# Batch 0's keys and queries made in the last tiles of a top-2 expert stage, and a chain of small VectorE steps spread between other work

## The chip, the cores and the metric

The kernel runs on one core of a Trainium2 chip. The metric is the device time of one execution in microseconds (us), as the median of several. TensorE (PE) multiplies matrices, VectorE (DVE), ScalarE (ACT) and GpSimd (POOL) do the elementwise work, and the queue of SyncE (SPq) issues the DMAs.

## The reference

Eight steps follow one another on x, 16 batches of 112 rows by 256 values. Even steps are cross-attentions to a context of 375 rows for each batch, odd ones are feed-forward steps. This case is about the places where a top-2 expert step hands over to the next attention.

```python
x = x + tanh(g_xattn[0]) * L0_xattn(layernorm(x), ctx, ...)   # 16 heads of 16
x = x + tanh(g_ffn[0])   * L0_ffn(layernorm(x), ...)          # 8 experts, the best 2 kept
x = x + tanh(g_xattn[1]) * L1_xattn(layernorm(x), ctx, mask)  # scores clipped to +-100, masked
x = x + tanh(g_ffn[1])   * L1_ffn(layernorm(x), ...)          # 8 experts, the best 2 kept
x = x + tanh(g_xattn[2]) * L2_xattn(layernorm(x), ctx)
...                                                           # three more steps
# an attention, for each batch
q, k, v = xn @ wq + bq, ctx @ wk + bk, ctx @ wv + bv
out = softmax(q k^T / 4, per head) @ v @ wo + bo
# a top-2 step: gates from the logits, all experts computed, two of them weighted
```

## The kernel before

The program is a sequence of stages: attention 0, top-2 stage 0, attention 1, top-2 stage 1, attention 2, and three others. Each stage is a block in which every engine has its own instruction stream, and each block ends in a barrier of all engines. An engine waits for another by semaphores; inside a stage all orders are written out by hand.

An attention handles one batch in a turn, with a software pipeline over batches: turn i has the exponentials and the weighing of batch i (`on["e"]`), the scores and row maxima of batch i+1 (`on["m"]`), the keys and queries of batch i+2 (`on["p"]`), and the output of batch i-1 (`on["o"]`). `schedule` runs turns -3 to 16. A turn has 32 slots, and a `Plan` says at which slot each piece stands. For turns below 0 (`start`) the pieces are not spread over the slots: the keys come first, then the queries, then all scores. Keys and queries go through DRAM to be laid out by heads: PE makes keys (two products of 6 matmuls, `keys`) and queries (`L1258`), ACT and POOL or DVE split them into two fp16 parts (`L812`, `L1013`; in attention 1 `L806`, `L717`, `L719`; the queries `L823`, `L731`, `L733`), SPq writes them (`L620`, `L630`) and reads them back as stacks (`kst` at `L574`, `qst` at `L578`), and only then can PE make scores (`L1184`). DVE takes each score's row maximum (`L1053` or `L1057`); at the end of the turn PE turns the maxima (`L1273`).

A top-2 stage works on 14 tiles of 128 rows, again skewed: in iteration i PE makes the eight experts' products of tile i in four groups of six matmuls (`experts`), the logits of tile i+1 and the transposes of tile i+2. ACT scales four experts, DVE adds the other four (`L1483`), POOL sums and writes tile i (`L1425`), DVE takes its statistics in iteration i+1 (`L1505`). Bank 1 of PSUM holds the logits only. The reciprocal standard deviations that the next layer norm needs come from a Newton iteration of 13 small dependent DVE steps (`rstd_part`, called in one go by `row_rstd`): once at the end of iteration 0 for the tiles 10 to 13, and once at the end of iteration 13 for the first 11 batches, with the shifts and the first two normed batches behind them. Iterations 1 to 10 are a hardware loop of two iterations a trip, the others stand unrolled.

## Time and profile before

| | us |
|---|---|
| median of 3 executions (lowest, highest) | 1503.87 (1501.83, 1505.4) |
| the profiled execution's own time | 1508.3 |
| its span, first to last instruction | 1506.5 |
| busy in it: PE, DVE, ACT, POOL | 1343.4, 1118.5, 689.8, 417.6 |

The difference between own time and span, 1.8 us, lies around the instructions. Busy time is summed over the whole span; stages differ, so the places of the change are read from the timeline, which gives the start of each group of instructions in us from the span's start. The handovers that matter here lie at 395.4 (to attention 1) and 862.7 (to attention 2), the starts of the two top-2 stages at 292.6 and 753.8.

### The profile page before, as it was taken

To read this page: it belongs to the slowest core of one execution; us is meant where nothing else is said; L and a number is where in the kernel's file an instruction comes from. 1 tells how busy PE (TensorE), PEld (TensorE's weight loads), DVE (VectorE), ACT (ScalarE), POOL (GpSimd) and SP (SyncE) were. 2 spreads that over 40 slices of the span, in tenths; PEclk is the share of its full clock that TensorE was granted. 3 is DMA by queue.
4 is the path that set the end of the run, shared out by engine and by line. 5 is a ranking of instruction groups with operands and counts; after the bars stand their busy time and mean duration, and the time that the engine had idled before them with its cause. 6 is when DMAs were issued, how large, how long until landed. Compare 5 with 4: busy or idle time off the path is not lost. (4 is left out here: it accounts for less than half of the span.)

```text
span 1506.5 us, 36868 instructions
## 1 busy us (share of the span) xinstructions
PE 1343.4 (89%) x11864; PEld 980.0 (65%) x11864; DVE 1118.5 (74%) x3709; ACT 689.8 (46%) x1635; POOL 417.6 (28%) x588
## 2 busy tenths in 40 slices
PE   5799999799689899999789779999987997996998
PEld 2577887545356676776534348787876886883766
DVE  7688787578489888888678757767664775666997
ACT  2566676533234455554333236667662222332331
POOL 2233336244433344446124413333330000000000
PEclk8899999899889999999889979999999998997999
DMA  5444445311323233334010233333335441451000
GB/s 158 119 133 119 138 144 156 92 69 32 97 83 92 73 86 89 90 87 116 15 56 18 68 98 96 91 101 89 101 124 166 141 160 35 123 150 34 11 17 21
DMA packets 134832, 138.80 MB, mean 92 GB/s; under 512 B 38601, under 2 KB 122060, under 8 KB 134604
## 3 DMA queue, kind: packets, MB, share of 16 engines
q1 hardware_dynamic: 134716, 137.30, 31.7%
q8 instruction: 67, 1.10, 0.3%
q14 instruction: 49, 0.40, 0.1%
HBM read 101.77 MB, written 35.48 MB: 91 GB/s over the span
## 5 line engine op out<-in xcount | busy, mean ns | idle before, releaser
L1057 DVE TENSOR_REDUCE negm<-ps 112x1 f32<-112x375 f32 x512 | 260.1, 541 | 114.2 <-PE ps L1184 112.4
L777 ACT ACTIVATE p<-ps 125x448 f32<-125x448 f32 x432 | 229.3, 543 | 189.0 <-PE ps L1212 118.0
L1184 PE MATMUL ps<-kst,qst 96*112 96x375 f16 x768 | 236.1, 343 | 21.3 <-DMA qst<-q_split 9.4
L1199 PE MATMUL ps<-qst,kst 112*125 112x224 f16 (+1 forms) x1152 | 211.6, 266 | 8.3 <-POOL qst L747 4.3
L747 POOL TENSOR_TENSOR qst<-m_row,diag 16x448 f16<-16x448 f16 x128 | 130.0, 1043 | 283.6 <-ACT m_row L851 278.6
L1199 PEld LDWEIGHTS ps<-qst,kst 112*125 112x125 f16 (+1 forms) x1152 | 149.1, 139 | 45.1 <-issue 9.5
L1613 PE MATMUL ps<-fw,xs_e 128*128 128x512 f16 x672 | 167.5, 390 | 0.0
L1053 DVE CUSTOM_DVE_ANT_0 with_mask<-ps,mask_add 112x375 f16<-112x375 f32 x256 | 135.8, 546 | 19.9 <-issue 18.5
L1041 DVE TENSOR_SCALAR ps<-ps 125x448 f32<-125x448 f32 x192 | 120.9, 630 | 29.0 <-PE ps L1199 27.5
L1184 PEld LDWEIGHTS ps<-kst,qst 96*112 96x112 f16 x768 | 99.0, 133 | 53.9 <-DVE negm L1057 25.6
L1107 PE MATMUL ps<-ctxT,wkv_split 128*128 128x375 f16 (+1 forms) x576 | 118.6, 348 | 9.8 <-DVE ctxT L888 9.2
L1107 PE MATMUL ps<-wkv_split,ctxT 128*125 128x256 f16 x864 | 119.0, 275 | 0.8 <-DVE ks L1013 0.8
L1223 PE MATMUL ps<-p,v 125*32 125x112 f32 x3456 | 113.6, 265 | 1.5 <-ACT p L777 0.9
L747 POOL TENSOR_TENSOR mst<-m_row,mask_diag 32x448 f16<-32x448 f16 x64 | 64.5, 1036 | 162.3 <-ACT m_row L851 154.6
L1613 PEld LDWEIGHTS ps<-fw,xs_e 128*128 128x128 f16 x672 | 65.3, 100 | 66.0 <-issue 6.5
L1107 PEld LDWEIGHTS ps<-wkv_split,ctxT 128*125 128x125 f16 (+1 forms) x864 | 97.9, 137 | 2.8 <-DVE ks L1013 0.7
L1223 PEld LDWEIGHTS ps<-p,v 125*32 125x32 f32 x3456 | 81.3, 111 | 26.0 <-issue 17.8
L1212 PE MATMUL ps<-mst,mask_add 128*125 128x448 f16 x192 | 74.1, 395 | 24.6 <-DVE ps L1041 23.7
L1107 PEld LDWEIGHTS ps<-ctxT,wkv_split 128*128 128x128 f16 x576 | 58.7, 104 | 47.8 <-issue 23.0
L777 ACT ACTIVATE p_a<-ps 125x448 f32<-125x448 f32 x144 | 78.0, 543 | 22.1 <-PE ps L1212 14.9
L2345 PE MATMUL ps<-wgu,xqT 128*128 128x512 f32 (+3 forms) x224 | 72.4, 478 | 3.4 <-DVE xh L2274 2.0
L860 ACT ACTIVATE v<-ps 125x256 f32<-125x256 f32 x144 | 55.7, 387 | 26.1 <-PE ps L1107 21.6
(237 smaller groups left out, 2409.8 us busy)
## 6 DMA issues: line engine op xcount, KB each, us to landing
k_split<-ks SPq DMA_DIRECT2D x48, 375.0 KB, 3.5
kst<-k_split SPq DMA_DIRECT2D x96, 187.5 KB, 2.9
fw<-in_w SPq DMA_DIRECT2D x16, 1024.0 KB, 7.2
qst<-q_split SPq DMA_DIRECT2D x96, 112.0 KB, 2.4
kst<-k_split SPq DMA_DIRECT2D x96, 93.8 KB, 2.6
stage<-in_ctxT SPq DMA_DIRECT2D x16, 375.0 KB, 4.3
ctxn<-in_ctx SPq DMA_DIRECT2D x16, 375.0 KB
rows<-x SPq DMA_DIRECT2D x48, 112.9 KB, 2.6
```

What stands on the lines that cost most here:

```text
L747: pool.tensor_tensor(m_stack[q][m_rows, 4 * hg:4 * hg + 4, :], g.m_row[q][m_rows, :].rearrange("p (o s) -> p o s", o=1) .to_broadcast([n_m ...
L777: act.activation(p[P_OF[hg]][:, kt, :], ps[0:KR, BK_ST + n % 2, 0:4 * S], ACT.Exp).then_inc(s_exp, 1)
L1041: dve.tensor_scalar(st, st, -CLIP, CLIP, ALU.max, ALU.min).then_inc(s_clip, 1)
L1053: dve.tensor_tensor_reduce(g.with_mask[h % 2][:, :], scored, g.mask_add[1 - par][0:S, :], 1.0, -3e38, ALU.add, ALU.max, g.maxima[1 - par][ ...
L1057: dve.tensor_reduce(g.negm[1 - par][:, h:h + 1], scored, AX_X, ALU.max, negate=True).then_inc(s_max, 1)
L1107: mm = pe.matmul(out, lhs(l, c), rhs(r, c), start=(k == 0), stop=(k == 3 * KC - 1))
L1184: mm = pe.matmul(ps[0:S, BK_S + h % 2, 0:SK], g.q_stack[q][0:96, h, :], g.k_stack[q][0:96, h // 2, :], start=True, stop=True)
L1199: mm = pe.matmul(bank[:, 2 * r * S:2 * (r + 1) * S], g.k_stack[par][0:rows, pr, kt * KR:(kt + 1) * KR], g.q_stack[par][0:rows, 2 * pr:2 * ...
L1212: pe.matmul(bank, g.mask_add[par][:, kt * KR:(kt + 1) * KR], g.m_stack[par][:, 4 * hg:4 * hg + 4, :], start=False, stop=True, skip_group_c ...
L1223: mm = pe.matmul(pv[32 * j:32 * j + 32, hg * S:(hg + 1) * S], g.v[par][:, kt, 4 * hg + j, :], p[P_OF[hg]][:, kt, j * S:(j + 1) * S], start ...
L1613: mm = pe.matmul(out, lhs(l, c), rhs(r, c), start=(k == 0), stop=(k == 3 * KC - 1))
L2345: mm = pe.matmul(gate_up[w][:, first:last], xqT[:, c, :], wgu[:, w, c, first:last], start=(c == 0), stop=(c == KC - 1))
```

## The change

Batch 0's part of the first turns of attention 1 and 2 moves into the top-2 stage before it: in iteration 11 and 12 (NT is 14) PE makes the two key products in bank 1 (the logits' bank), in iteration 12 it turns batch 0's normed rows and in iteration 13 it makes the queries, with their copies, splits and DMA writes. The attention then begins at turn -1, with its pieces at the plan's slots, since `start` holds for attention 0 alone. The semaphores for these steps are shared by the stages (`FirstBatch`). The 13 steps of each `rstd` chain stand one by one at five places of each iteration, from iteration 0 (tiles) and from iteration 9 (batches 0 to 7 rather than 0 to 10). DVE makes the low half of the next tile (`xs`) before it finishes the gate weights, ACT copies the turned weights before it makes the exponentials, the split of the key and value weights moves from iteration 12 to 10, and the hardware loop covers iterations 3 to 8.

```diff
-        for i in range(-3, 5):
+        for i in range(-3 if first else -1, 5):
...
+                for e in range(2):
+                    sp.wait_ge(s_qdram[0][e], 16)
+                for c in range(2):
+                    stack_queries(sp, g, 0, c, s_stack[0][c])
                 read_batches(sp, g, layer - 1, 2, NT)
...
-                start = isinstance(i, int) and i < 0
+                start = first and isinstance(i, int) and i < 0
...
# top-2 stage, SyncE
+                    if isinstance(i, int) and i == NT - 1:
+                        held(sp, g, n0.khi, 2)
+                        held(sp, g, n0.klo, 2)
+                        store_keys(sp, g, 0, n0.kdram[0])
...
+                    if isinstance(i, int) and i == NT:
+                        held(sp, g, n0.qsplit, 1)
+                        for e in range(2):
+                            store_queries(sp, g, 0, e, n0.qdram[0][e])
+                        sp.wait_ge(n0.kdram[0], 16)
+                        for c in range(2):
+                            stack_keys(sp, g, 0, c, n0.stack[0][c])
...
# top-2 stage, VectorE
+                def part_of_rstd(i, k):
...
+                    first = 0 if i < 3 else NT - 5
+                    n = (i - first) * 5 + k
+                    if not 0 <= n < RSTD_PARTS:
+                        return
...
+                    if isinstance(i, int) and i in (NT - 3, NT - 2):
+                        m = i - NT + 3
+                        dve.wait_ge(n0.khi, m + 1)
+                        dve.scalar_tensor_tensor(out=g.k_split[0][:, m, 1, :], in0=ps[:, 1, 0:SK],
+                                                 scalar=g.bk[:, m:m + 1], in1=g.k_split[0][:, m, 0, :],
+                                                 op0=ALU.add, op1=ALU.subtract).then_inc(n0.klo, 1)
...
# top-2 stage, TensorE
                     if tiled(i + 1):
                         pe.wait_ge(s_xlo, i + 2)
+                        if isinstance(i, int) and i == NT - 2:
+                            pe.wait_ge(n0.klo, 1)
...
+                    if isinstance(i, int) and i in (NT - 3, NT - 2):
+                        m = i - NT + 3
+                        pe.wait_ge(s_wlo, 1)
+                        pe.wait_ge(s_lgsb, i + 2)
+                        split_products(ps[:, 1, 0:SK], lambda l, c: g.wkv_split[:, 0, l, c, m * 128:(m + 1) * 128],
+                                       lambda r, c: g.ctxT[:, r, c, 0:SK]).then_inc(n0.k, 1)
```

PE's instructions at the handover to attention 1, before: behind the last experts (`fw`) the barrier, the bias product (`wo,bv`), the keys (`ctxT,wkv_split`), transposes (`ident,xn`) and queries (`xnT,wq`).

```order
L1096 MATMUL ps<-wo,bv 1x256 [waits attention_weights1]
L1096 MATMUL ps<-wo,bv 1x256
L1107 MATMUL ps<-ctxT,wkv_split 128x375 x12
L1150 MATMUL ps<-ident,xn 128x112 [waits a0_bias_copied,a0_x_loaded3]
L1150 MATMUL ps<-ident,xn 128x112
L1258 MATMUL ps<-xnT,wq 128x112 [waits a0_ident]
L1258 MATMUL ps<-xnT,wq 128x112 x3
L1107 MATMUL ps<-ctxT,wkv_split 128x375 [waits a0_q_split]
```

These are the keys and queries of batch 0 and the first keys of batch 1; the scores (`L1184`, `kst,qst`) come 12 rows further on.

And the same place now:

```order
L1135 MATMUL ps<-wo,bv 1x256 [waits attention_weights1]
L1135 MATMUL ps<-wo,bv 1x256
L1223 MATMUL ps<-kst,qst 112x375 [waits a_stacked0_0]
L1189 MATMUL ps<-ident,xn 128x112 [waits a_q_scaled,a0_bias_copied,a_xn]
L1189 MATMUL ps<-ident,xn 128x112
L1146 MATMUL ps<-ctxT,wkv_split 128x375 x6
L1223 MATMUL ps<-kst,qst 112x375
L1223 MATMUL ps<-kst,qst 112x375 [waits a0_experts_high]
L1146 MATMUL ps<-ctxT,wkv_split 128x375 x6
L1223 MATMUL ps<-kst,qst 112x375 [waits a0_experts_high] x2
L1297 MATMUL ps<-xnT,wq 128x112 [waits a_xnT]
```

Batch 0's first score stands right behind the bias product, and batch 1's keys and queries between batch 0's scores.

PE's instructions in iterations 11 and 12 of top-2 stage 0 now; `gws_e` are logits, `expert_b` the bias of the experts:

```order
L1769 MATMUL ps<-expert_b,gates_T 128x256 [waits e0_bias_added,e0_weights_copied]
L1721 MATMUL ps<-ctxT,wkv_split 128x375 [waits e0_logits_biased,e0_keys_low]
L1721 MATMUL ps<-ctxT,wkv_split 128x375 x5
L1721 MATMUL ps<-fw,xs_e 128x512 [waits e0_accumulated]
L1721 MATMUL ps<-fw,xs_e 128x512 x5
L1790 MATMUL ps<-ident,xn 128x128 [waits e0_x_low,e0_xn]
L1790 MATMUL ps<-ident,xn 128x128
L1721 MATMUL ps<-fw,xs_e 128x512 [waits e0_expert_scaled]
L1721 MATMUL ps<-fw,xs_e 128x512 x5
L1721 MATMUL ps<-gws_e,xs_e 128x8 [waits e0_logits_biased,a_k_low,e0_x_low]
```

Before, nothing stood between the bias and the fourth group of experts, and the logits did not wait for `a_k_low`.

DVE's instructions in an early iteration now, where the low half of the next tile (`xs_e`) stands ahead of the last two gate-weight steps and a step of the chain (`newton`) between the last two additions:

```order
L1682 SCALAR_TENSOR_TENSOR w_e<-iota,indexf_e,ex_e 128x8
L1687 TENSOR_TENSOR xs_e<-ps,xs_e 128x256 [waits e0_x_high]
L1691 TENSOR_TENSOR w_e<-w_e 128x8 [waits e0_dve]
L1695 TENSOR_SCALAR weight_e<-w_e,rden_e 128x8 [waits e0_dve]
L1562 SCALAR_TENSOR_TENSOR part_e<-ps,weight_e,part_e 128x256 [waits e0_dve,e0_expert]
L291 TENSOR_SCALAR newton<-newton 128x4 [waits e0_dve]
L1562 SCALAR_TENSOR_TENSOR acc_e<-ps,weight_e,part_e 128x256 [waits e0_dve,e0_expert]
```

Before, `xs_e` was the third of these, and all `newton` steps followed `acc_e`.

## Rows read from the trace of the kernel before

**Rows 1.** The page: busy time, share of the span, instructions.

```profile
PE 1343.4 (89%) x11864; PEld 980.0 (65%) x11864; DVE 1118.5 (74%) x3709; ACT 689.8 (46%) x1635; POOL 417.6 (28%) x588
```

**Rows 2.** Windows: the header, steady tiles of top-2 stage 0, batch 0's scores.

```profile
core 0: us, PE busy (x) PEld busy (x) DVE busy (x) ACT busy (x) POOL busy (x), PEclk, DMA share, GB/s
330.00:348.00 18.00, 18.00 (x103) 8.93 (x102) 15.14 (x84) 7.07 (x24) 7.97 (x11) 1.00 0.06 22
...
412.20:422.70 10.50, 8.06 (x16) 2.60 (x16) 8.47 (x50) 0.00 (x0) 0.00 (x0) 0.50 0.63 177
```

**Rows 3.** Timeline, entry of attention 1 (start, duration, engine, line, operation, [idle before]).

```profile
395.54 1.87 PE L1096 MATMUL ps<-wo,bv 128*1 128x256 f32 x4 [6.64 <-PEq L1376]
...
404.72 1.33 SPq L630 DMA_DIRECT2D q_split<-qs  x2
...
408.09 1.12 SPq L574 DMA_DIRECT2D kst<-k_split  x2
...
412.25 0.88 PE L1184 MATMUL ps<-kst,qst 96*112 96x375 f16 x2 [4.00 <-DMA qst<-q_split]
...
422.71 0.37 PE L1273 MATMUL ps<-ident,maxima 112*32 112x112 f32 x1 [0.86 <-DVE maxima L1064]
...
423.24 0.52 PE L1184 MATMUL ps<-kst,qst 96*112 96x375 f16 x1
```

**Rows 4.** Timeline, entry of attention 2.

```profile
862.78 1.87 PE L1096 MATMUL ps<-wo,bv 128*1 128x256 f32 x4 [7.02 <-PEq L1376]
...
878.83 0.88 PE L1184 MATMUL ps<-kst,qst 96*112 96x375 f16 x2 [2.95 <-DMA qst<-q_split]
...
893.02 0.83 PE L1184 MATMUL ps<-kst,qst 96*112 96x375 f16 x2
```

**Rows 5.** Timeline, tiles 0 and 1 of both top-2 stages.

```profile
306.05 0.73 POOL L1425 TENSOR_TENSOR packed<-p,acc_e 128x256 f32<-128x256 f32 x1 [2.85 <-DVE acc_e L1483]
306.08 0.72 DVE L285 TENSOR_SCALAR newton<-newton 128x4 int32<-128x4 int32 x1
...
310.88 0.80 PE L1651 MATMUL ps<-expert_b,gates_T 128*128 128x256 f32 x2 [2.63 <-ACT gates_T L1458]
...
311.47 2.77 PE L1613 MATMUL ps<-fw,xs_e 128*128 128x512 f16 x6
...
316.71 0.73 POOL L1425 TENSOR_TENSOR packed<-p,acc_e 128x256 f32 x1 [3.84 <-DVE acc_e L1483]
...
772.35 1.22 PE L1651 MATMUL ps<-expert_b,gates_T 128*128 128x256 f32 x2 [2.72 <-ACT gates_T L1458]
```

**Rows 6.** Timeline, steady tiles of top-2 stage 0, then of stage 1.

```profile
321.41 0.42 DVE L1588 TENSOR_TENSOR xs_e<-ps,xs_e 128x256 f16<-128x256 f32 x1
...
341.82 0.73 POOL L1425 TENSOR_TENSOR packed<-p,acc_e 128x256 f32 x1 [2.27 <-DVE acc_e L1483]
...
348.11 0.72 POOL L1425 TENSOR_TENSOR packed<-p,acc_e 128x256 f32 x1 [2.27 <-DVE acc_e L1483]
...
798.66 0.72 POOL L1425 TENSOR_TENSOR packed<-p,acc_e 128x256 f32 x1 [2.82 <-DVE acc_e L1483]
...
804.42 0.30 PE L1613 MATMUL ps<-gws_e,xs_e 128*128 128x8 f16 x6 [0.26 <-DVE xs_e L1588]
...
805.47 0.72 POOL L1425 TENSOR_TENSOR packed<-p,acc_e 128x256 f32 x1 [2.82 <-DVE acc_e L1483]
```

**Rows 7.** Timeline, end of top-2 stage 0.

```profile
390.45 0.74 POOL L1425 TENSOR_TENSOR packed<-p,acc_e 128x256 f32<-128x256 f32 x1
...
393.84 0.42 DVE L1505 BATCH_NORM_STATS2 stats<-packed 128x6 f32<-128x256 f32 x1
```

**Rows 8.** Timeline, attention 1: transposes, queries, keys, each for one batch.

```profile
400.60 0.36 PE L1150 MATMUL ps<-ident,xn 112*128 112x112 f32 x2
...
402.39 2.08 PE L1107 MATMUL ps<-ctxT,wkv_split 128*128 128x375 f16 x12
...
405.11 1.15 PE L1258 MATMUL ps<-xnT,wq 128*128 128x112 f32 x8 [0.45 <-ACT xnT L797]
```

More of the change, by code:

```diff
@@ L33 @@
 EPS = 1e-5
-SEM_SET = 66
+SEM_SET = 67
 ROWS = 128
@@ L762, in _ @@
             if biased:
-                act.wait_ge(s_w, 16 * n_w)
-                step(act.activation(g.bq[:, :], g.bq[:, :], ACT.Copy, scale=SCALE))
                 act.wait_ge(s_bvo, 1)
```

221 lines of the change are left out of this document (151 added, 70 removed).

## The prediction

> **What bounds the kernel now.** I read the page first: PE is busy 89% of the span [rows 1], DVE 74%. No engine fills the span, so I looked at the places of the change one by one.
>
> Inside the top-2 stages, the windows show PE without a gap at a granted clock of 1.00, 2.4 GHz, and DVE busy 15.14 of 18.00 us [rows 2]. The timeline shows that the two are nearly balanced in stage 0: a tile takes 348.11 - 341.82 = 6.29 us, and DVE's one wait in it is for POOL's update, which itself follows DVE's last addition. In stage 1 a tile takes 805.47 - 798.66 = 6.81 us, and PE's logits wait for DVE's `xs_e` [rows 6]; there DVE's loop through POOL decides.
>
> The entries of attention 1 and 2 are chains. Attention 1 begins at 395.54. Batch 0's queries are issued to DRAM at 404.72, the stacks are read from 408.09, the first score runs at 412.25, the maxima are turned at 422.71 and batch 1's first score, which opens turn 0, is at 423.24: 27.7 us from the first instruction [rows 3]. In attention 2 the same three points are 862.78, 878.83 and 893.02: 30.2 us [rows 4]. While batch 0's scores run alone, PE's clock is granted at 0.50, 1.2 GHz, and DVE has 8.47 us of work in 10.50 [rows 2].
>
> Two smaller holes lie in the top-2 stages. In tile 0 the 13-step chain stands ahead of tile 1's gates: PE waits 2.63 us for the copied weights and runs the next group of six matmuls in 2.77 us, at about half the rate of a steady group. POOL's updates are then 316.71 - 306.05 = 10.66 us apart. Stage 1 has the same wait, 2.72 us [rows 5]. At the end, POOL has written tile 13 at 390.45 + 0.74 = 391.19, but DVE takes its statistics at 393.84, behind the second chain [rows 7].
>
> **The change part by part, both top-2 stages together unless said.**
>
> (a) The chain leaves tile 0. The tile there cost 10.66 against 6.29 us: -4.4. In stage 1 the tile is 6.81 us; with a like interval of 10.7 it gives -3.9 (the interval is taken from stage 0, since the wait is alike). Together -8.3.
>
> (b) The 26 steps of a stage are paid elsewhere. Tile 0's five stand where DVE waits for PE anyway. Of the other iterations' five places, the one before the statistics and the one after the last addition are covered by DVE's wait for POOL. Three a full iteration, 13 a stage, are not covered. In tile 0 the 13 of them lengthened the next tile by 4.4 us at most, 0.34 a step, part of it PE's lowered clock; nothing if hidden. I take 0.2 us for a step, between the two: 26 x 0.2 = +5.2. A step that meets POOL took 0.72 us [rows 5]; if four in ten do, as POOL is busy 7.97 of 18.00 us [rows 2], this is 26 x 0.4 x 0.5 = 5 us more. If they all slip into waits it is 0. I take 5.2 since most steps of a chain beside POOL would still be quick ones.
> The Trainium skill, SBUF — State Buffer, section on who interferes with whom, says that a DVE instruction with two SBUF inputs and a GpSimd one that reads SBUF exclude each other for a whole instruction. By that rule nearly every such meeting would cost up to a POOL addition, and the sum would be up to some 8 us worse. The row of 0.72 us agrees for one step, whose neighbours in the same chain it leaves open.
>
> (c) The chain leaves the tail. The statistics can follow POOL at 391.2 rather than at 393.84: -2.7 in each stage, -5.4.
>
> (d) `xs_e` stands ahead of two gate-weight steps. In stage 1 the logits wait 0.26 us for it in a tile [rows 6], and it now comes sooner by those two steps: -0.2 us in each of 12 tiles, -2.4. In stage 0 PE doesn't wait for it; ACT's high half sets its start, 321.41 in the row, so that DVE waits there first and the two steps come behind it. Its next addition was at most a `xs_e` of 0.42 behind [rows 6], so a tile could get 0.35 longer, or nothing changes if DVE's wait for POOL takes it up. PE decides the tile there; I take 0. Bounds for both stages: -3.1 (0.26 x 12) to +8.4 (0.35 x 24). ACT's earlier copy of the turned weights takes a wait from PE, nothing more.
>
> (e) PE's new work in iterations 11 to 13, where PE has no gap. Keys 2.08, transposes 0.36, queries 1.15 [rows 8]: 3.6 a stage by modelled ends, 3.4 from start to start: +6.8. What is behind it on PE are the fourth expert group and then the transposes of the next tile; ACT's and POOL's parts of tile 12 follow PE by more than a us and stay covered. The copies on ACT and the query split on POOL end before tile 13's last addition. SPq gets eight more DMAs: the keys' write and the mask ahead of the store of tile 12, two query writes and four key reads ahead of the store of tile 13. The two query writes are issued in 1.33 us and two key reads in 1.12 [rows 3], about 4 us for the six from the query split on, which stands three expert groups (4 us) before the end of PE's work, while the statistics come some 3 us after it. Without that cover the store of tile 13, and with it the barrier, would be late by up to 4 us.
>
> (f) The bank. Tile 13's logits use bank 1 and now wait for DVE's low half of key product 0, which stands behind `acc_e` of tile 11. Counted from the start of tile 13's transposes: PE gets to the logits at +1.5, DVE starts `xs_e` at +0.8, then two gate steps, two additions and the low half, and ends at +3.0 to 3.1. PE waits 1.6, and with it all its experts behind: +3.2 for both stages. Covered below by nothing; above, the clock may be lowered after it as in tile 1, 1.4 us each: range 0 to 6.
>
> Stages: -8.3 + 5.2 - 5.4 - 2.4 + 6.8 + 3.2 = -0.9.
>
> (g) The entries. Times from the first PE instruction. In attention 1 a score came 4.2 us after the start of four stack reads, two of keys and two of queries [rows 3]. Now SPq issues only the query reads first, and score 0 runs at about 3.4 (before: 16.7). Batch 1's keys and queries stand between the scores. A key product of six matmuls takes 2.08 / 2 = 1.0 at full clock [rows 8] and about 1.9 at half. PE from 3.4 on: score 0 0.3, transposes 0.4, keys 1.9, two scores 0.6, keys 1.9, two scores 0.6, queries 1.1 to 2.1: 10.2 to 11.2. Copy and split 2.5, so the queries are issued at about 12.5 to 13.7. From there the known chain holds: 408.09 - 404.72 = 3.4 to the stack reads and 412.25 - 408.09 = 4.2 to a score [rows 3], so turn 0 opens at 20 to 21.3. Batch 0's scores took 422.71 - 412.25 = 10.5 alone; with the 3.6 to 5.5 of PE work between them they are done at 17.5 to 19.4, so batch 1's stack decides. Against 27.7: -6.4 to -7.7. I take -7.0. In attention 2 the queries stand earlier, the stack is there at about 17.6, and batch 0's scores decide: 3.4, then the 893.02 - 878.83 = 14.2 us that lay between the two batches' first scores [rows 4], and the same work between them, of which 3.4 to 5 shows: 21 to 22.5. Against 30.2: -7.7 to -9.2, I take -8.5. The clock is why there are two ends: keys between the scores run at 1.2 GHz if it stays at 0.50 as in [rows 2]. Together -15.5.
> The Trainium skill, TensorE: Matmul & The Clock Gate, Part 1, says that the throttled state is the default and activity releases it. The window of the scores shows no release in its 10.5 us, at 8.06 us of PE work [rows 2]. By the rule turn -1, which has more matmuls than the scores alone, would be released, and the entries would give some 1.5 us more each.
>
> The move of attention 1's and 2's own chain (eight batches rather than five, at slots 12 to 24) and of the weight split costs nothing: DVE executes the same 13 steps, and POOL's split in iteration 10 has DVE's additions ahead of it. Uncovered, 2.3 us of POOL once a stage.
>
> **Sum.** -0.9 - 15.5 = -16.4 us. The sum is made against the profiled execution's own 1508.3: 1491.9. That one stood 4.4 us above the median of 1503.87, so the median becomes 1503.87 - 16.4 = 1487.5.
>
> **Rivals.**
> 1. Batch 1's stack is later than I count. The entries give half, 8 us: its keys and queries now share PE and the SPq queue with the scores. For it: in attention 1 the stack is already what decides. Against it: the chain's pieces come from rows. Total -0.9 - 8 = -9: 1495. Chance 0.10.
> 2. Slower: DVE's new order lengthens every tile. Place: `xs_e` waits for ACT and everything behind it, gate weights, additions, POOL's update. Price: 0.35 of waiting plus 0.55, the excess of a 0.72 us step over a short one [rows 5], when the gate steps now fall on POOL's additions, 0.9 us x 26 tiles = +23; 1503.87 - 16.4 + 2.4 + 23 = 1513. It decides from 0.7 us a tile. Against: DVE's wait for POOL moves along with its additions, but its 15.14 of 18.00 us [rows 2] leaves it nearly 1 us a tile. Chance 0.05.
> 3. More than forecast: the bank's wait is hidden, the chain steps slip into waits and the clock is released in turn -1: -3.2 - 5.2 - 3 more: 1476. Chance 0.08.
> 4. The stages give back most of the entries, through steps at POOL's price (b, +5), a lowered clock after the bank's wait (f, +2.8) and the upper half of (d): no change, 1502. Chance 0.03.
> The forecast has 0.74 and by its bounds 1480 to 1494.
>
> **Numbers.** Leaving out 1476's lower half and rivals 2 and 4, the range is 1478 to 1497. About 0.2% (3 us) is what can be told from no change. Faster 0.92 (forecast, 1, 3), same 0.03, slower 0.05.
>
> **What the new profile would show.** (a) POOL's first two updates of a top-2 stage 6.2 to 7.5 us apart, and no 2.6 us wait of PE for the turned weights. (b, d) steady tiles of 6.2 and 6.7 us; 6.9 and more would be rival 2. (c) the last statistics within 0.3 us of POOL's update. (f) a PE wait of about 1.6 us at tile 13's logits. Top-2 stages of nearly unchanged length, within 2 us. (g) the first score 3 to 4 us after the attention's first matmul, batch 1's first score at 20 to 21.3 and 21 to 22.5 us. Batch 1's later than 24 is rival 1. Wrong altogether I would be if the attention's later turns got longer.

## The result and the profile after

| | us |
|---|---|
| kernel before, median of 4 executions | 1502.85 (1499.62 to 1505.4) |
| changed kernel, median of 4 | 1464.45 (1461.52 to 1466.26) |
| ratio, 95% interval | 0.9759 (0.9724 to 0.9794) |
| profiled execution: own time, span | 1464.46, 1462.7 |

The change makes the kernel 38.4 us faster. I forecast 16.4 us, and the result is outside the range of 1478 to 1497. Measured twice more, the changed kernel gave 0.9762 (0.9734 to 0.9789) and 0.9761 (0.9736 to 0.9787).

To find the difference I cut the span at rows that both kernels have: POOL's update of tile 0, the first matmul of each attention after a top-2 stage, and the turning of turn 0's maxima. "Update" is the row in which POOL writes a tile; an entry runs from an attention's first matmul to the turning of turn 0's maxima. (The forecast counted an entry to batch 1's first score, where turn 0 opens.) Two profiles of before and three of the changed kernel, all of them unchanged code, stand side by side.

| stretch, us | before | changed | means differ | forecast |
|---|---|---|---|---|
| start to update of tile 0, stage 0 | 306.1, 303.8 | 300.4, 303.3, 300.9 | -3.4 | 0 |
| top-2 stage 0, update of tile 0 to the next first matmul | 89.5, 89.6 | 88.5, 87.3, 86.9 | -2.0 | stages -0.9 |
| entry of attention 1, first matmul to turn 0's maxima | 49.4, 50.5 | 38.9, 39.5, 38.9 | -10.9 | -7.0 |
| attention 1 from there, to update of tile 0, stage 1 | 322.6, 321.0 | 314.3, 314.4, 313.5 | -7.7 | 0 |
| top-2 stage 1 | 95.3, 95.3 | 90.3, 90.4, 92.1 | -4.3 | (as above) |
| entry of attention 2 | 45.0, 45.0 | 33.0, 32.7, 34.0 | -11.8 | -8.5 |
| rest | 598.7, 597.5 | 597.2, 595.0, 597.1 | -1.7 | 0 |

The first line is no effect: its code is unchanged, and over all profiles of this study that stretch took from 299.8 to 306.1 us in kernels of either sort.

The page's busy line of the changed kernel answers to [rows 1]. The span is 43.8 us shorter. PE's busy time fell by 24.3 of them for the same 11864 matmuls, at a mean granted clock of 0.959 rather than 0.947, and its idle time by 19.5 (the ends of matmuls are modelled); DVE's busy time fell by 12.9 us for the same 3709 instructions. So more than half of the gain is the same work done in less time, not waits that went.

```profile
PE 1319.1 (90%) x11864; PEld 974.2 (67%) x11864; DVE 1105.6 (76%) x3709; ACT 692.6 (47%) x1635; POOL 413.8 (28%) x580
```

The timeline of the entry of attention 1 in the changed kernel answers to [rows 3]: first matmul, batch 0's first score, batch 1's two key products, its queries, their writes and key reads on SPq, batch 0's maxima turned, batch 1's first score.

```profile
388.91 1.86 PE L1135 MATMUL ps<-wo,bv 128*1 128x256 f32 x4 [3.69 <-PEq L1417]
...
392.21 0.56 PE L1223 MATMUL ps<-kst,qst 96*112 96x375 f16 x1 [1.44 <-DMA qst<-q_split]
...
392.94 2.09 PE L1146 MATMUL ps<-ctxT,wkv_split 128*128 128x375 f16 x6
...
395.33 1.12 PE L1146 MATMUL ps<-ctxT,wkv_split 128*128 128x375 f16 x6
...
396.67 1.04 PE L1297 MATMUL ps<-xnT,wq 128*128 128x112 f32 x8
...
400.14 1.35 SPq L403 DMA_DIRECT2D q_split<-qs  x2
...
403.59 1.12 SPq L410 DMA_DIRECT2D kst<-k_split  x2
...
404.44 0.27 PE L1312 MATMUL ps<-ident,maxima 112*32 112x112 f32 x1 [0.48 <-DVE maxima L1107]
...
407.56 0.37 PE L1223 MATMUL ps<-kst,qst 96*112 96x375 f16 x1 [2.65 <-DMA qst<-q_split]
```

The reader is to see the two key products: the same six matmuls take 2.09 and then 1.12 us, so the clock rose between them. Batch 0's first score stands at 3.3 us as forecast (3.4), the query writes at 11.2 (12.5 to 13.7), the maxima at 15.5 (17.5 to 19.4), batch 1's first score at 18.65 (20 to 21.3; before 27.7). In attention 2 batch 0's first score came at 4.65 us, later than the 3 to 4 us that I had named, and batch 1's at 18.45 (21 to 22.5; before 30.2). The windows over both entries say the same of the clock. They answer to the third row of [rows 2], where it was 0.50; the second and the fourth window here hold batch 0's scores (the fourth with all that stands ahead of them in attention 2; from 837.1 us on, where the scores begin, the clock was 0.92), the third and the fifth turn 0.

```profile
core 0: us, PE busy (x) PEld busy (x) DVE busy (x) ACT busy (x) POOL busy (x), PEclk, DMA share, GB/s
388.90:392.20 3.30, 1.86 (x4) 0.34 (x4) 0.48 (x2) 0.37 (x1) 0.00 (x0) 0.50 0.52 120
392.20:404.40 12.20, 10.41 (x56) 6.79 (x56) 8.52 (x50) 3.14 (x8) 4.05 (x9) 0.88 0.33 90
404.40:427.80 23.40, 17.90 (x165) 12.50 (x166) 19.22 (x70) 9.20 (x21) 8.24 (x13) 0.93 0.33 92
832.50:847.90 15.40, 12.37 (x54) 6.65 (x54) 9.20 (x19) 3.73 (x9) 1.10 (x3) 0.79 0.32 87
847.90:865.50 17.60, 14.45 (x178) 10.86 (x179) 11.20 (x25) 9.72 (x22) 5.11 (x7) 1.00 0.39 108
```

The line of 7.7 us is the one I had priced at nothing. Windows from one turning of the maxima to the next show it: in the kernel before, the one that ends turn 2 of attention 1 takes 19.31 us, the next two 23.04 and 24.06. The chain's steps of turns 2 and 3 stand in the last slots there, so that they run just behind these turns' maxima, in the two long windows. The last line is the first long window in the second profile of before: 21.4 us, at a clock of 1.00 and not 0.93. The second fence has the last of the chain's steps, with the shift behind them, beside POOL's four additions to the M stack.

```profile
464.29:483.60 19.31, 18.33 (x202) 13.57 (x200) 16.94 (x71) 10.43 (x25) 8.09 (x13) 1.00 0.33 90
483.60:506.64 23.04, 20.20 (x203) 14.42 (x200) 20.17 (x78) 10.55 (x25) 8.37 (x13) 0.93 0.27 76
506.64:530.70 24.06, 20.18 (x202) 14.31 (x200) 21.11 (x78) 10.54 (x25) 8.13 (x13) 0.93 0.26 72
...
482.62:504.07 21.45, 18.56 (x203) 13.51 (x200) 20.09 (x78) 10.46 (x25) 8.39 (x13) 1.00 0.30 82
```

```profile
507.43 0.17 DVE L296 SCALAR_TENSOR_TENSOR newton<-newton 112x5 f32<-112x5 f32 x1
507.57 4.00 POOL L747 TENSOR_TENSOR mst<-m_row,mask_diag 32x448 f16<-32x448 f16 x4 [10.29 <-ACT m_row L851]
507.63 1.00 DVE L291 TENSOR_TENSOR newton<-newton 112x5 f32<-112x5 f32 x1
508.66 0.96 DVE L293 TENSOR_TENSOR newton<-newton 112x5 f32<-112x5 f32 x1
509.65 0.95 DVE L296 SCALAR_TENSOR_TENSOR rstd<-newton 112x5 f32<-112x5 f32 x1
510.64 0.96 DVE L309 SCALAR_TENSOR_TENSOR row_shift<-x,rstd 112x5 f32<-112x5 f32 x1
```

A step of 0.17 us takes 1.00 as soon as POOL works, four of them for four additions of 1.0 us, 3.2 us more than alone. In the first long window three steps meet POOL (0.88, 0.95 and 0.95 us), 2.3 us more than alone. The windows grew by 3.7 and 4.8 us at a clock of 0.93, the first by 2.1 us where the clock stayed at 1.00. So the steps' length explains 2 and 3 us, and a lowered clock that followed in some executions some 1.6 us a window. The changed kernel's windows that hold the chain, those of turns 2 and 3:

```profile
447.17:466.63 19.46, 18.48 (x202) 13.58 (x200) 17.24 (x76) 10.58 (x25) 8.09 (x13) 1.00 0.32 93
466.63:486.11 19.48, 18.50 (x203) 13.59 (x200) 17.49 (x78) 10.52 (x25) 8.11 (x13) 1.00 0.32 86
```

In the top-2 stages, POOL's first two updates (to [rows 5]) are 6.09 us apart in stage 0, and 748.67 - 742.17 = 6.50 in stage 1. Steady tiles take 6.34 us on average in stage 0, as 6.08 and 6.61 mostly in turn, and 6.60 in stage 1 (I had named 6.2 and 6.7). The tail, from POOL's last update to the attention's first matmul, answers to [rows 7]: that update and the statistics, which now follow it at once.

```profile
300.38 0.72 POOL L1485 TENSOR_TENSOR packed<-p,acc_e 128x256 f32<-128x256 f32 x1 [2.91 <-DVE acc_e L1562]
...
306.47 0.72 POOL L1485 TENSOR_TENSOR packed<-p,acc_e 128x256 f32<-128x256 f32 x1 [2.37 <-DVE acc_e L1562]
...
386.40 0.72 POOL L1485 TENSOR_TENSOR packed<-p,acc_e 128x256 f32<-128x256 f32 x1 [1.88 <-DVE acc_e L1562]
387.17 0.42 DVE L1584 BATCH_NORM_STATS2 stats<-packed 128x6 f32<-128x256 f32 x1 [0.84 <-issue]
```

The bank's wait is there, and longer than I counted. PE waited 2.01 us in stage 0 and 2.87 in stage 1 where I had 1.6. The timeline of tiles 11 and 12 of stage 0 has POOL's weight split, a chain step that met it (1.11 us; in stage 1 1.12), the next low half, the key's low half, and PE's logits 2.01 us late with a group of six at half rate behind them; the window (second fence) shows the lowered clock.

```profile
363.65 2.32 POOL L1489 TENSOR_TENSOR wkv_split<-wkv,wkv_split 128x512 f16<-128x512 f32 x2
...
364.88 1.11 DVE L295 TENSOR_TENSOR newton<-newton 112x8 f32<-112x8 f32 x1
...
368.70 0.41 DVE L1687 TENSOR_TENSOR xs_e<-ps,xs_e 128x256 f16<-128x256 f32 x1
...
370.34 0.60 DVE L1704 SCALAR_TENSOR_TENSOR ks<-ps,bk,ks 128x375 f16<-128x375 f32 x1
...
371.04 0.29 PE L1721 MATMUL ps<-gws_e,xs_e 128*128 128x8 f16 x6 [2.01 <-issue]
371.19 2.64 PE L1721 MATMUL ps<-fw,xs_e 128*128 128x512 f16 x6
```

```profile
370.50:379.60 9.10, 8.56 (x41) 4.22 (x42) 5.40 (x31) 2.20 (x7) 2.90 (x4) 0.81 0.22 57
```

### The profile page after: what moved, and what is told of

It reads as the page before. It is cut to its first block and busy times, and to the rows that moved or that the text cites. A ratio compares the mean times of both kernels' runs of the same rounds, so it can differ in the third digit from the quotient of the medians.

```text
span 1462.7 us, 36540 instructions
## 1 busy us (share of the span) xinstructions
PE 1319.1 (90%) x11864; PEld 974.2 (67%) x11864; DVE 1105.6 (76%) x3709; ACT 692.6 (47%) x1635; POOL 413.8 (28%) x580
## 3 DMA queue, kind: packets, MB, share of 16 engines
q1 hardware_dynamic: 134716, 137.30, 32.7%
## 5 line engine op out<-in xcount | busy, mean ns | idle before, releaser
L1223 PE MATMUL ps<-kst,qst 96*112 96x375 f16 x768 | 229.9, 335 | 17.2 <-DVE negm L1100 8.9
L1223 PEld LDWEIGHTS ps<-kst,qst 96*112 96x112 f16 x768 | 97.8, 131 | 45.3 <-DVE negm L1100 21.6
L1146 PE MATMUL ps<-ctxT,wkv_split 128*128 128x375 f16 (+1 forms) x552 | 109.3, 337 | 8.8 <-DVE ctxT L922 8.2
L1262 PEld LDWEIGHTS ps<-p,v 125*32 125x32 f32 x3456 | 80.9, 110 | 25.7 <-issue 17.6
L1146 PEld LDWEIGHTS ps<-ctxT,wkv_split 128*128 128x128 f16 x552 | 54.5, 101 | 40.5 <-issue 15.0
```

The costliest lines, as they stand in the source:

```text
L1146: mm = pe.matmul(out, lhs(l, c), rhs(r, c), start=(k == 0), stop=(k == 3 * KC - 1))
L1223: mm = pe.matmul(ps[0:S, BK_S + h % 2, 0:SK], g.q_stack[q][0:96, h, :], g.k_stack[q][0:96, h // 2, :], start=True, stop=True)
L1262: mm = pe.matmul(pv[32 * j:32 * j + 32, hg * S:(hg + 1) * S], g.v[par][:, kt, 4 * hg + j, :], p[P_OF[hg]][:, kt, j * S:(j + 1) * S], start ...
```

## The experiments

Each ratio is to the kernel before, measured beside the run. Lengths of stretches come from each run's own profile.

**The attentions' own chain** (the kernel before beside these runs: 1499.1 us). First the kernel before once more, unchanged.

> The kernel before, unchanged, profiled once more. The changed kernel's attention 0, whose code is the same, was 5.5 us shorter in its profile. Theory: that is from execution to execution, and this profile will show a first top-2 stage that starts within 288 to 293 us, somewhere between the two kernels' 287.3 and 292.9. Rival: the change does something to attention 0; then the start stands at 292.9 again, within 0.5 us.

Its own time was 1504.53; its stretches are the second column of the first table. The first top-2 stage's update of tile 0 came at 303.8 us, 2.3 sooner than in the first profile; the runs below had it at 299.8 to 305.2. So the 5.7 us of attention 0 between the first two profiles are mostly from execution to execution, and nothing shows the change in them. The other thing that this run shows is the first long window of attention 1 at 21.4 us, with the same three long steps as in the first profile, where it took 23.0.

```diff
# b1_even: kernel before, DVE in attention 1 and 2 (CALM is 25 in attention 1)
-                if not first and i in (2, 3):
-                    n = (s - CALM) + (0 if i == 2 else SLOTS - CALM)
+                if not first and i in (2, 3) and 12 <= s < 26 and s % 2 == 0:
+                    n = (s - 12) // 2 + 7 * (i - 2)
...
```

> The kernel before with one edit: the own chain of attention 1 and 2 stands at the even slots 12 to 24 of turns 2 and 3, as in the changed kernel, not at the last slots. Theory: in the last slots its steps meet POOL's four additions of 1.0 us that follow the turned maxima, and turns 2 and 3 of attention 1 took 23.04 and 24.06 us where 19.4 is regular. With the edit both take 19.4 to 19.7: -8 us, and -1.4 in attention 2, -9.5 together, 1493 to 1494 us. The prediction's position (rival): the same steps cost the same wherever they stand; no change, 1502 to 1505 us.

1491.4 us, ratio 0.9940 (0.9920 to 0.9961). The three windows from turn 1's maxima to turn 4's took 19.46, 19.47 and 19.31 us, 58.2 together, where they had taken 66.4 in the first profile of before and 64.8 in the second: a gain of 8.2 or 6.6. One window of attention 2 took 14.97 where it had taken 16.59, 1.6 more. These 8.2 to 9.8 us are as expected; in the medians 7.7 us shows.

```diff
# b2_row: kernel before
+                if not first and i in (2, 3) and 12 <= s < 19:
+                    n = (s - 12) + 7 * (i - 2)
...
```

> The kernel before with the chain of attention 1 and 2 at the slots 12 to 18 of turns 2 and 3, one step a slot and in a row as before, seven slots that end before POOL's additions to the M stack begin. Theory (the meeting with POOL costs, not the density): turns 2 and 3 of attention 1 take under 20.5 us, total -8 us, near 1495 us. Rival (seven dependent steps in consecutive slots delay the row maxima behind them, wherever they stand): turns 2 and 3 stay at 22 us and more, no gain over 3 us.

1497.18 us, 0.9973 (0.9956 to 0.9990). In the median 1.9 us of the 8 expected show, and the interval leaves them out; why this version's executions came out longer than those of the one above stays open. The stretches are clear: the windows with the chain took 19.60 and 19.61 us and the one behind them 19.31, 58.5 together. The rival had expected 22 us and more. Windows of this run:

```profile
464.31:483.91 19.60, 18.58 (x202) 13.54 (x200) 17.39 (x78) 10.66 (x25) 8.11 (x13) 1.00 0.34 94
483.91:503.52 19.61, 18.59 (x202) 13.56 (x200) 17.38 (x78) 10.55 (x25) 8.11 (x13) 1.00 0.33 88
```

The same steps in a row, in other slots, cost 0.3 us a turn, against the 19.31 of a turn without them. Its profiled execution (1499.32) stood 2 us above its median.

```diff
# a1_late: changed kernel
-                if not first and i in (2, 3) and 12 <= s < 26 and s % 2 == 0:
-                    n = (s - 12) // 2 + 7 * (i - 2)
+                if not first and i in (2, 3) and 25 <= s < 32:
+                    n = (s - 25) + 7 * (i - 2)
```

> The changed kernel with one edit: the own chain of attention 1 and 2 stands at the slots 25 to 31 of turns 2 and 3, seven in a row as it did before, still for eight batches. Theory: turns 2 and 3 of attention 1 take 23 to 24 us again, +8 to +9 with attention 2's part, 1473 us. Rival (the entries' new timing, not the slots, removed the long turns): no change, 1463 to 1466 us.

1470.02 us, 0.9806 (0.9779 to 0.9833), where the changed kernel is at 0.976: 23.08 and 23.97 us for the two windows again, at a clock of 0.93, and in the second steps of 0.99, 0.96, 0.96 and 0.95 us beside POOL's four additions. Attention 2's windows stayed at 14.96 us both, though one step in the one and two in the other met POOL there (0.89, 0.98 and 0.96 us): an excess of up to 1.6 us disappeared in DVE's waits. In the kernel before, four steps met it in one window of attention 2, 3.2 us over their own length, and 1.6 of it showed, at a clock of 1.00. The theory had 8 to 9 us with attention 2's part; attention 1 alone gave 8.1.

**The top-2 stages and the entries** (the kernel before beside these runs: 1502.08 us). "Updates 0 to 10" is the time from the update of tile 0 to that of tile 10.

```diff
# c1_xs_after: changed kernel, DVE in the top-2 stage; xs_e moves down
-                        dve.tensor_tensor(xs[par][:, 1, :, :], turned, xs[par][:, 0, :, :], ALU.subtract)
...
                         step(dve.tensor_tensor(w1[:, :], w1[:, :], w2[:, :], ALU.add))
...
                         dve.tensor_scalar(w[q][:, :], w1[:, :], rden[:, 1:2], None, ALU.mult).then_inc(s_wt, 1)
+                        dve.tensor_tensor(xs[par][:, 1, :, :], turned, xs[par][:, 0, :, :], ALU.subtract)
```

> The changed kernel with DVE's two old places exchanged again: the next tile's low half (xs_e) stands behind the sum and the scaling of the gate weights, as before. By the prediction's term (d): stage 1's steady tiles go from 6.60 back to 6.8 us, stage 0's stay at 6.3: +2.4 in all, 1472 to 1473 us on this chip, where a sister of the changed kernel took 1470.0. Rival (stage 1's shorter tiles come from ACT's earlier copy of the turned weights): the tiles stay at 6.60, no change.

1470.57 us, 0.9785 (0.9748 to 0.9822). Stage 1's steady tiles took 6.68 us: neither 6.8 nor 6.60. Updates 0 to 10 took 63.7 and 66.4 us in the two stages against 62.8 and 65.5 in the changed kernel, +1.9 together. (d)'s sum of -2.4 nearly holds, but half of it is in stage 0, where I had put nothing. Batch 1's keys ran wholly at the lower clock in the entry of attention 1 (2.09 us each), which took 41.2 us.

```diff
# c2_klo_early: changed kernel; the key product's low half, with its wait, moves up
+                        dve.scalar_tensor_tensor(out=g.k_split[0][:, m, 1, :], in0=ps[:, 1, 0:SK],
...
                         dve.tensor_tensor(xs[par][:, 1, :, :], turned, xs[par][:, 0, :, :], ALU.subtract)
...
                         add_expert(i, par, 7, added)
                     part_of_rstd(i, 4)
-                        dve.scalar_tensor_tensor(out=g.k_split[0][:, m, 1, :], in0=ps[:, 1, 0:SK],
```

> The changed kernel with DVE's low half of the key products ahead of the next tile's xs_e, not behind the tile's last addition. Theory (term (f) was too small: PE idled 2.0 us ahead of tile 13's logits in stage 0 and 2.9 in stage 1, and ran the group behind the first wait at 1.2 GHz): the wait shrinks by 1.3 to 1.4 us in each stage, and the slow group with it: -2.7 to -4.5 us. Rival (POOL's split of the key and value weights made DVE late, so the wait only changes its releaser): less than 1 us.

1466.65 us, 0.9775 (0.9739 to 0.9811), not told from the changed kernel, where 2.7 to 4.5 us less were expected. PE waited 0.67 us at tile 13's logits in stage 0 and 1.50 in stage 1, there for `xs_e`, and no slow group followed. Updates 10 to 13 took 20.4 and 21.1 us, not 21.7 and 22.4, -1.3 in each stage. But the tail grew from 2.51 to 3.68 and 3.23 us. SyncE's queue shows why, in this run's timeline:

```profile
379.58 0.35 SPq L246 DMA_DIRECT2D x<-rows  x1
380.29 0.39 SPq L398 DMA_DIRECT2D k_split<-ks  x1
...
384.21 1.65 SPq L403 DMA_DIRECT2D q_split<-qs  x2
387.36 2.29 SPq L410 DMA_DIRECT2D kst<-k_split  x4
389.75 0.38 SPq L229 DMA_DIRECT2D rows<-packed  x1
```

The key reads stand ahead of the last store and are issued only 7.1 us after the key write, which went out behind a read of x. The cover of which the prediction spoke (the statistics 3 us behind PE) was used up.

```diff
# c3_one_go: changed kernel, DVE; no steps of part_of_rstd below iteration 3
+                    if isinstance(i, int) and i == 0:
+                        row_rstd(dve, g, step, rows, TILES_READ[1][0], NT)
```

> The changed kernel with the tiles' chain in one go at the end of iteration 0, as before; everything else as changed. By terms (a) and (b): the second tile takes 10.6 us again and not 6.1 to 6.5, +4.3 in each stage, +8.6 in all, of which the spread steps give back what they cost: by (b)'s 0.2 us a step half of 5.2, so +6. Theory after the result (the spread steps cost nothing in tiles 1 and 2, since tiles 1 to 3 took 12.68 us against 12.56): the full +8.5.

1469.14 us, 0.9779 (0.9719 to 0.9838). Both sizes missed: the second tile took 8.43 and 8.97 us, 2.3 and 2.5 more than in the changed kernel, and updates 0 to 10 were 2.5 and 2.3 us longer. So beside the new orders of DVE and ACT the chain costs only about half of the 4.4 us that the second tile had over a steady one. In the profiled execution tile 12 took 9.1 and 8.9 us at a clock of 0.81; the four executions spread from 1462.65 to 1477.63 us, so the stretches tell more than the median.

```diff
# c4_unspread: changed kernel, PE and DVE in the attentions
-                start = first and isinstance(i, int) and i < 0
+                start = isinstance(i, int) and i < 0
```

> The changed kernel with turn -1 of attention 1 and 2 unspread, as before: batch 1's keys and queries first, then batch 0's 16 scores together; batch 0's keys and queries stay in the top-2 stage. Theory: batch 0's scores run at a granted clock of 0.50 again and take 10.5 and about 14 us from some 7 us on; the maxima are turned at 18 and 21 us after the attention's first matmul, not at 15.5 and near 15; turn 0 then doesn't wait for the stack. +2 to +3 us an entry, +5 in all. Rival (only batch 1's stack counts, and its queries now leave 1 to 2 us sooner): no change, or 1 us less an entry.

1473.74 us, 0.9795 (0.9745 to 0.9845). The maxima came at 17.7 and 19.1 us. The entries took 39.8 and 38.5 us against 39.1 and 33.2: +0.7 and +5.3. In attention 2, 3.8 of it stand ahead of the maxima; the rest is turn 0, which ran at a clock of 0.81 there (19.4 us; 17.3 and 17.6 at a clock of 1.00 in two of the changed kernel's profiles, 18.6 at 0.86 in the third). Batch 1's first score came at 18.25 us in attention 1, no later than with the spreading (18.65 to 19.3), and at 23.15 in attention 2 (18.45 to 19.4). So the moved parts alone shorten the entries by 10.1 and 6.5 us. Windows of this run over attention 1's scores and over attention 2's entry:

```profile
399.00:407.60 8.60, 6.12 (x15) 2.00 (x16) 8.17 (x49) 0.00 (x0) 0.00 (x0) 0.76 0.61 163
...
834.30:853.40 19.10, 15.97 (x54) 6.99 (x54) 9.68 (x19) 3.51 (x9) 1.10 (x3) 0.68 0.45 119
```

**ACT's order, and a better version** (the kernel before beside the first, the third and the fourth run: 1503.19 us).

```diff
# c5_act_order: changed kernel, ACT in the top-2 stage
-                        act.activation(wT[0:E, :], ps[0:E, 3, 0:ROWS], ACT.Copy).then_inc(s_wTsb, 1)
                         act.activation(ex[:, :], lg[:, :], ACT.Exp, bias=neg[:, 0:1],
                                        accum_out=den[:, 0:1]).then_inc(s_ex, 1)
+                        act.activation(wT[0:E, :], ps[0:E, 3, 0:ROWS], ACT.Copy).then_inc(s_wTsb, 1)
```

> The changed kernel with ACT's two old places exchanged again: the exponentials of the next tile's gates first, then the copy of the turned weights. The prediction counted this edit as nothing. Theory after the runs so far: with the tiles' chain put back the second tile cost 2.3 to 2.5 us, not the 4.1 to 4.6 that the change took off it, and with DVE's order put back stage 1's tiles took 6.68, not 6.82; the rest of both is ACT's order. Then this run has second tiles of about 8 us and steady tiles of 6.75 in stage 1: +5 to +6 us. Rival (ACT's copy only shares the gain with the other two edits, each alone being enough): under +1 us.

1471.41 us, 0.9801 (0.9768 to 0.9834). The second tile took 6.39 and 6.65 us, not 8; but every steady tile was longer, 6.67 us in stage 0 and 6.75 in stage 1, and updates 0 to 10 by 2.8 and 1.5 us.

The next edit is the reverse of this diff, made in the kernel before (b4_act_alone; an earlier form of it, b3_act_alone, gave no time).

> The kernel before with ACT's new order alone: the copy of the turned weights ahead of the exponentials. With the order undone in the changed kernel, steady tiles of both stages went to 6.67 and 6.75 us and the second tiles only to 6.39 and 6.65. Theory (ACT's order is worth something by itself, wherever DVE's chain stands): the second tile of each top-2 stage takes 8.4 to 9.5 us and not 10.6, stage 1's steady tiles 6.7 and not 6.82: -3 to -5 us. Rival, the prediction's count: the edit alone is worth nothing, within 1 us, and only pays beside DVE's new order.

1499.85 us against 1502.05, 0.9985 (0.9957 to 1.0012), not told from no change. Its profile: second tiles of 9.50 and 9.47 us (10.66 and 10.6 before), steady tiles of 6.66 in stage 1 (6.82) but of 6.15 and 6.68 in turn in stage 0 (6.29). The changed kernel's alternate there too, in most tiles (6.08 and 6.61), and with the order undone in it they do not (6.65 to 6.68): the alternation goes with ACT's order in both kernels. Updates 0 to 10: +1.3 us in stage 0, -2.6 in stage 1. Alone the edit is worth 1.3 us, as the last of three 4.3.

```diff
# d1_better: c2_klo_early, and on SyncE in iteration 14 (and POOL's wv split in iteration 11)
-                        for c in range(2):
-                            stack_keys(sp, g, 0, c, n0.stack[0][c])
+                        stack_keys(sp, g, 0, 0, n0.stack[0][0])
# at the attention's start
+                stack_queries(sp, g, 0, 0, s_stack[0][0])
+                stack_keys(sp, g, 0, 1, s_stack[0][1])
+                stack_queries(sp, g, 0, 1, s_stack[0][1])
```

> The changed kernel with three edits: the key products' low halves ahead of xs_e; two of the four key reads of batch 0 (the second half of the stack) moved from the end of the top-2 stage to the start of the attention, behind the first query reads; and POOL's split of the value weights an iteration later than that of the key weights. Theory: the first edit took the wait at tile 13's logits from 2.0 and 2.9 us to 0.7 but moved the end to the SPq queue, whose 2.29 us of key reads stood ahead of the last store (3.68 us from the last update to the next stage's first matmul, not 2.51); with half of them gone the tail is 2.6 again, and DVE is no longer held by 2.3 us of POOL in one tile. -2.5 to -4 us against the changed kernel, and no slow group behind the logits. Rival (the tail waits for something else, a DMA's completion): the tail stays at 3.5 and the version is within 1 us of the one with the first edit alone.

1463.95 us, 0.9736 (0.9708 to 0.9765). Stages of 86.3 and 89.0 us, but tails of 3.60 and 2.99: the key reads waited 1.9 us for the key write, which landed 7.5 us after its issue. The rival was right on the tail. POOL's split in two halves brought a little: PE waited 0.33 and 0.93 us at tile 13's logits, not 0.67 and 1.50, and updates 10 to 13 took 20.1 and 20.5 us, not 20.4 and 21.1. The version below that keeps it and the one that leaves it out show the same difference.

> The changed kernel, unchanged, on the same chip and in the same call as the version above, to compare the two, and for a second profile: the first top-2 stage should start anywhere between 287 and 293 us, and tile 12 of stage 0 take 7.4 or 9.1 us, as in its sisters, at a granted clock of 1.00 or 0.81.

1466.51 us, 0.9762 (0.9734 to 0.9789): 2.6 us above the version with three edits, with overlapping intervals. Tile 12 took 7.4 us in both stages.

```diff
# d2_keys_first: d1_better, and on SyncE in iteration 13 (the read was ahead of the write)
                         store_keys(sp, g, 0, n0.kdram[0])
                         if layer == 0:
                             sp.dma_start(g.mask_in[0][0:S, :], a["mask"][0, :, :]).then_inc(n0.maskin[0], 16)
+                        read_batches(sp, g, layer, 1, i - 1)
```

> The version with three edits, and a fourth: in the last iteration of the top-2 stage the SPq queue writes batch 0's keys before it reads the batches 8 to 12 back, not behind. In the version with three edits the last store waited behind the key reads, and these 1.9 us for the landing of the key write, which came 7.5 us after its issue, behind a read of 564 KB; a key write lands after 3.7 us in the median. Theory: the key reads start as soon as the query writes are issued, and the tail (last update to the next stage's first matmul) takes 2.5 to 2.7 us, not 3.60 and 2.99: -1.4 us against the version with three edits. Rival (the landing is late for another reason): the tail stays.

1464.45 us against 1502.05, 0.9766 (0.9728 to 0.9804). The tails are 2.50 and 2.48 us, the stages 84.8 and 88.5, the shortest of all: the theory of the landing holds. But the entry of attention 1 took 41.5 us, with both key products at 1.2 GHz, and the ratio is no better than the changed kernel's.

The last version, d3_two_edits, is the changed kernel with the edit of c2_klo_early and the one just shown.

> The changed kernel with two edits alone: the key products' low halves ahead of xs_e, and in the last iteration of the top-2 stage the key write ahead of the read of batches 8 to 12. All key reads stay in the stage and the attention's start is the changed kernel's own. The version with four edits had the shortest stages (84.75 and 88.46 us from the first update to the next stage's first matmul; the changed kernel 87.35 and 90.37 in its second profile) but a slower entry into attention 1: its first score came at 4.1 us, not 3.3 to 3.5, and both key products behind it ran at 1.2 GHz. Theory (the slow entry came from the reads moved there): stages as short, entries of 39 and 33 us, -4 us against the changed kernel, 1461 to 1462. Rival (the clock of an entry falls either way whatever the queue does): stages as short, but an entry of 41 us again in one of the two, -2 us.

1462.33 us against 1500.73, 0.9756 (0.9728 to 0.9783). Stages of 85.5 and 89.0 us, entries of 40.9 and 32.8. The first score came at 3.8 us, and the clock rose only behind the second key product, as this run's timeline shows:

```profile
390.13 0.56 PE L1223 MATMUL ps<-kst,qst 96*112 96x375 f16 x1 [1.97 <-DMA qst<-q_split]
...
390.86 2.09 PE L1146 MATMUL ps<-ctxT,wkv_split 128*128 128x375 f16 x6
...
393.37 2.09 PE L1146 MATMUL ps<-ctxT,wkv_split 128*128 128x375 f16 x6
```

The reads that the version before moved are not needed for a slow entry; the rival holds. Nor does the time of the first score decide it: c2_klo_early had it at 3.8 us too, and its second key product took 1.38 us.

> The changed kernel, unchanged, in the same call, to be compared with the version of two edits: 1464 to 1467 us by both theories. Its third profile shows once more what the same code does in attention 0, tile 12 and the entries: 7.4 or 9.1 us for tile 12 of each stage.

1464.87 us, 0.9761 (0.9736 to 0.9787). Tile 12 took 7.4 us in stage 0 and 9.1 in stage 1. The version with two edits is 2.5 us faster in the medians and its intervals overlap: likely better, not shown.

## Why the prediction was wrong

**The step that failed most** is the last of the working: "The move of attention 1's and 2's own chain (eight batches rather than five, at slots 12 to 24) ... costs nothing: DVE executes the same 13 steps". The count of steps was right, their length was not. Shown from both sides: moved alone, the chain gave attention 1 back 8.2 us (6.6 against the second profile of before) and attention 2 1.6; put back, it took attention 1's again; and in a row at other slots it cost 0.3 us a turn. Each long step lasts as long as one POOL addition, up to 1.0 us. Three and four of them in a window of attention 1 are more than DVE's waits take up, and PE's clock was then granted at 0.93 in one of the two windows or in both, which took some 1.6 us more each. With this, 7.7 and 1.7 of the 22 us missing are explained, by the first table's means.

I had the mechanism in hand, at (b), and weighed it only for the top-2 stages. The Trainium skill, SBUF — State Buffer, section on who interferes with whom, has a DVE instruction with two SBUF inputs and a GpSimd one that reads SBUF exclude each other for a whole instruction; the four rows of 0.95 to 1.00 us agree with it. The up to 8 us that I worked out by it did come, but in the attentions, where I did not look, and not in the top-2 stages. The row of 0.72 us that I called agreement at (b) is none: it is a tensor_scalar with one input. The long turns were in the trace of before: 19.3, 23.0, 24.1, 19.5 us in a row. I never listed the turns' lengths. The same sentence put the weight split at nothing. It did meet a step of the stage's chain, and in two halves it was worth 0.3 and 0.6 us.

**(g), the entries,** the largest mis-sized term: -15.5 counted, -10.9 and -11.8 = -22.7 measured. Up to batch 1's first score, which is what I counted, it is -9.2 for -7.0 in attention 1 and -11.5 for -8.5 in attention 2. The skeleton was right: batch 0's first score at 3.3 us, in attention 1 batch 1's stack decides (PE waits 2.65 us for it), in attention 2 it hardly does (0.79 us). The excess has two parts that rows show. The clock: I counted the keys between the scores at 1.2 GHz and took the 10.5 us of the scores as they were at 0.50; it was granted at 0.88 and 0.92 on average over them, and in attention 1 the query writes left 1.3 to 2.5 us sooner (my lower end was itself 0.2 too low: 10.2 and 2.5 make 12.7). The Trainium skill, TensorE: Matmul & The Clock Gate, Part 1, which I cited, says that activity releases the throttled state; the second key product at 1.12 us agrees, but with a chance of 0.08 for rival 3 I hardly believed it. The trace of before had the sign: at its entry of attention 1 batch 0's two key products took 2.06 and 1.57 us and batch 1's 1.12 each. And I ended the account at batch 1's first score: turn 0 behind it was 1.4 us shorter too in attention 1 (20.3 from that score to the next maxima, 21.7 before, and 21.6 again without the spreading). How the excess splits between clock and spreading is only partly shown: without the spreading attention 2's entry lost 5.3 us, attention 1's 0.7. The clock's part is argued from the rows; no run changes it alone.

**The stages:** -0.9 counted, -6.3 measured, with a tail that is as counted.
- (c) -5.4 counted; tails of 5.09 and 4.87 us became 2.51 and 2.51, -4.9. Right.
- (a), (b), (d) and ACT's order lie in the updates 0 to 10: 67.2 and 72.1 us before, 62.8 and 65.5 after, -11.1. Undone one at a time, the tiles' chain costs 4.7, DVE's order 1.9, ACT's order 4.3: 10.9. That the three add up is partly luck, since the worth of ACT's order depends on the others. (a) with the spread steps of the tiles' chain is -4.7, where I had -8.3 and half of (b)'s 5.2, -5.7 together: close by chance, since the first is 3.6 too large and the second isn't seen. (d) is -1.9 of -2.4; and "ACT's earlier copy of the turned weights takes a wait from PE, nothing more" was worth 4.3. It is worth that beside the others only: alone it gave 1.3.
- (b)'s 0.2 us a step is not seen for the tiles' chain: updates 0 to 2 of stage 0, with eight steps among them, took 12.2 us, no more than two steady tiles, and the step of 0.72 us that met POOL behind each of these updates fell into DVE's wait.
- (e) and (f): updates 10 to 13 grew by 4.5 and 4.1 us, by 6.2 and 5.8 when the clock fell; counted were 5.0 a stage and steps of (b). (f) was 2.0 and 2.9 us of waiting, not 1.6: DVE came late, in both stages behind a chain step that had met POOL's weight split. With the low half moved ahead the waits were 0.67 and 1.50.
- The six DMAs on SPq stayed covered, with nothing to spare: as soon as the wait was shortened, they set the end (3.68 us).

**The rivals.** Rival 3 (more gain) named the released clock and the hidden steps, and both came, the steps in the tiles' chain at least; its third condition, a hidden wait for the bank, did not. It had 11.4 us more gain than the forecast, 22 were measured, and what is missing in it is the attentions' own chain and ACT's order. Rivals 1, 2 and 4 did not occur; with all changes stage 0's steady tiles went from 6.28 to 6.34 us on average, not up by 0.9. Later turns that get longer, my sign of being wrong altogether, did not show: they got shorter.

**What stays open.** What decides whether the clock falls behind tile 13's logits (7.4 or 9.1 us for the same code) and when it rises in an entry, and why it fell in one long window of attention 1 in some executions only. Why ACT's order makes stage 0's tiles alternate. Why the chain in a row gained only 1.9 us in the median. Whether the two-edit version is faster.

## What to carry to other kernels

List the lengths of all repetitions of a loop or turn before pricing an edit: one that is longer than its neighbours names a cost that the edit may remove or bring. In this kernel small dependent VectorE steps were priced by what GpSimd did in the same slots, not by their number; put them where GpSimd is idle or where VectorE waits anyway. When work is moved into a wait, look at which clock the engine runs at there, and at what is left of each cover behind it.

## What the runs showed of the hardware

- A DVE step on 112 x 5 values took 0.15 to 0.17 us alone and 0.88 to 1.00 beside POOL additions of 1.0 us, one for one. In the top-2 stages steps took 0.72 beside additions of 0.72, and 1.11 beside a split of 1.16 each; a tensor_scalar step of the chain with one input took 0.72 there too [rows 5].
- The same code at the same place ran at two clocks from execution to execution: tile 12 at 1.00 (7.4 us) or 0.81 (8.8 to 9.1), turn 0 of attention 2 at 1.00 (17.3 to 17.6 us) or 0.81 to 0.86 (18.6 to 19.7), and the second key product of attention 1's entry, over the changed kernel and its versions, in 1.12 to 2.09 us. In the kernel before, one window of attention 1 took 21.4 us at 1.00 or 23.0 at 0.93. That is 1 to 2 us each, and as much as the two versions that I tried at the end could gain.
- A key write of 375 KB landed 3.7 us after its issue in the median of d1_better, and once, at the end of its top-2 stage 0, after 7.5 us, when a read of 564 KB had been issued just ahead of it on the same queue. With the two exchanged the stages' tails went from 3.60 and 2.99 to 2.50 and 2.48 us.
